# Repacking the small products ahead of a recurrence: strips on TensorE, projections by mixed blocks, another order of banks

## The reference, cut to what matters

```python
# block 1: cross-attention over 375 context rows, 16 heads of 32, and an MLP of 2048
hidden = softmax(q @ k.T * scale) @ v @ cproj_w + cproj_b + x
x = hidden + gelu(layer_norm(hidden) @ fc_w + fc_b) @ proj_w + proj_b
# block 2
xa = _ln(x, ln1_w, ln1_b)
sx = previous row of xa - xa
xxx = tanh((xa + sx * maa_x) @ maa_w1).reshape(b, l, 5, 32)
xxx = einsum('blfd,fde->blfe', xxx, maa_w2)
xm = xa + sx * (maa_stack + xxx)
xk, xw, xv, xr, xg = the five of xm
w = exp(-exp(time_decay + tanh(xw @ td_w1) @ td_w2))      # td_w1: 512 x 64
r, k, v = xr @ Wr.T, xk @ Wk.T, xv @ Wv.T
g = silu(xg @ Wg.T)
# 32 heads of 16: out_t = r_t (u k_t v_t + s), s = k_t v_t + w_t s
x1 = x + group_norm(out) * g @ Wo.T
rr = sigmoid(xr2 @ Wfr.T); kk = square(relu(xk2 @ Wfk.T))  # xk2, xr2: mixes of ln(x1)
return x1 + rr * (kk @ Wfv.T)
```

## Time and profile before

| | |
|---|---|
| median of 3 runs | 1780.87 us |
| the profiled execution | 1791.03 us, span 1789.2 us |
| mean granted TensorE clock | 0.969 |
| TensorE busy | 1697.5 us (95%) |
| VectorE busy | 1167.6 us (65%) |
| ScalarE (ACT) busy | 657.2 us (37%) |
| GpSimd (POOL) busy | 281.2 us (16%) |

### The profile page before, as it was taken

One profiled execution on the slowest core, in us unless ns is written; L12 is line 12 of the kernel. 1 busy time (PEld: TensorE's weight loads), 2 busy tenths in 40 slices (PEclk: granted clock), 3 DMA queues, 4 the chain that ended last, 5 costly groups with the idle time before them and its releaser, 6 DMA issues.

```text
span 1789.2 us, 18450 instructions
## 1 busy us (share of the span) xinstructions
PE 1697.5 (95%) x6792; PEld 860.0 (48%) x6792; DVE 1167.6 (65%) x1620; ACT 657.2 (37%) x1507; POOL 281.2 (16%) x377
## 2 busy tenths in 40 slices
PE   6999999899999999999999999999989999999968
PEld 3555544345555444445555444455544445444423
DVE  1233200336999895548997965389989767999841
ACT  2466420124666222236663213256532135313111
POOL 1100000122121001121220002211200023136020
PEclk9999999889999999989999999999999999999989
DMA  7001012124111123351120232520022415232131
GB/s 254 12 29 52 1 52 90 50 83 141 37 45 54 41 93 127 97 159 37 37 62 22 88 114 89 157 78 9 16 76 78 135 52 159 85 118 74 56 101 44
DMA packets 75143, 138.82 MB, mean 78 GB/s; under 512 B 16624, under 2 KB 26736, under 8 KB 75056
## 3 DMA queue, kind: packets, MB, share of 16 engines
q1 hardware_dynamic: 60064, 102.36, 17.8%
q0 software_dynamic: 11776, 31.70, 6.0%
q10 hardware_dynamic: 3216, 3.60, 0.7%
HBM read 113.78 MB, written 23.86 MB: 77 GB/s over the span
## 4 chain that ended last, share of the span: by engine, by line
PE 82%; DVE 11%; issue 3%; ACT 3%; ACTq 1%; POOL 0%; DVEq 0%; POOLq 0%
PE bank L324 55%; PE bank L511 12%; PE bank L366 4%; PE bank L358 3%; PE bank L596 3%; DVE C L1315 2%; PE bank L378 2%; DVE sm L1252 1%; PE bank L631 1%; PE bank L346 1%; DVE C L1323 1%; DVE YB L1332 1%; PE bank L610 1%; DVE C L1307 1%; ACT XA L988 1%
## 5 line engine op out<-in xcount | busy, mean ns | idle before, releaser
L1315 DVE TENSOR_TENSOR_SCAN C<-XA,C 128x896 f32<-128x896 f32 x112 | 228.8, 2043 | 3.2
L511 PE MATMUL bank<-ring,HT 128*112 128x512 f32 x512 | 222.3, 592 | 0.0
L1252 DVE CUSTOM_DVE_ANT_0 sm<-bank,maskb 112x375 f32<-112x375 f32 x256 | 124.4, 542 | 139.0 <-PE bank L358 138.5
L324 PE MATMUL bank<-ctx_t,Wk 128*128 128x375 f32 x512 | 200.1, 517 | 14.3 <-DMA Wk<-in_wk 11.3
L324 PE MATMUL bank<-C,ring 128*128 128x448 f32 x512 | 209.2, 565 | 1.4 <-ACT Wk L988 1.4
L324 PE MATMUL bank<-SX,ring 128*128 128x448 f32 (+2 forms) x544 | 195.9, 519 | 4.1 <-issue 4.1
L324 PE MATMUL bank<-Wv,ctx_t 128*125 128x512 f32 x384 | 180.9, 596 | 0.4 <-ACT C L988 0.4
L366 PEld LDWEIGHTS bank<-ident,sm 112*125 112x125 f32 x768 | 124.8, 191 | 106.5 <-ACT sm L1003 44.1
L1009 ACT ACTIVATE probT<-bank 125x336 f32<-125x336 f32 x256 | 114.1, 446 | 164.3 <-PE bank L366 162.7
L1003 ACT ACTIVATE sm<-sm,nm 112x375 f32<-112x375 f32 x256 | 153.4, 599 | 3.3 <-DVE nm L1252 3.1
L511 PEld LDWEIGHTS bank<-ring,HT 128*112 128x112 f32 x512 | 90.6, 177 | 127.2 <-issue 127.2
(11 more groups left out here) (166 smaller groups left out, 2156.3 us busy)
## 6 DMA issues: line engine op xcount, KB each, us to landing
ring<-in_stream SPq DMA_DIRECT2D x64, 1024.0 KB, 5.2
ctx_t<-in_ctxT SPq DMA_DIRECT2D x16, 750.0 KB, 4.7
rkw_scratch<-HT POOLq DMA_DIRECT2D x48, 224.0 KB, 3.1
rkw<-rkw_scratch POOLq DMA_DIRECT2D x24, 224.0 KB, 3.2
HT<-in_x SPq DMA_DIRECT2D x16, 224.0 KB, 5.5
X<-in_x SPq DMA_DIRECT2D x16, 224.0 KB, 5.1
v_scratch<-HT POOLq DMA_DIRECT2D x16, 224.0 KB, 2.7
VB<-v_scratch SPq DMA_DIRECT2D x4, 896.0 KB, 4.5
```

Of the source, the lines that this page charges most:

```text
L324: last_ = nc.tensor.matmul(out_ap, pairs[k][0], pairs[k][1], start=(k == 0), stop=(k == len(pairs) - 1))
L511: last_ = nc.tensor.matmul(bank[SC[b]][0:LQ, :], HT[:, c, b * LQ:(b + 1) * LQ], w[:, c, :], start=(m == 0 and c == 0), stop=(m == 3 and c ...
L1252: nc.vector.tensor_tensor_reduce(out=sm[0:LQ, slot, :], in0=tile(name)[0:LQ, 0:LK], in1=maskb[:, n % 2, :], scale=-SCALE, scalar=3.0e38, o ...
L1315: own.step(nc.vector.tensor_tensor_scan(out=part, data0=wrep[:, i % 2, :], data1=part, initial=0.0, op0=ALU.mult, op1=ALU.add))
```

## The change

- W1 is cut into 80 products of 32 output rows by 112 columns: for each of the five factors j the four sequences go to four column strips of the array and lie under one another in one bank. The tanh is five instructions of 128 x 112 into TA.
- `low_rank(j)` is 16 products (4 sequences in 4 row strips, 4 blocks of channels), of 112 columns, with one bank for each sequence. `maa_w2` is repeated four times down the partitions; three of its five factors are loaded for each group by SP into memory lent by `sm` or `qT`.
- TD and DC go in two strips of 64, each with 224 columns.
- VectorE scales in 16 pieces of 112 columns for a mix. Mixes 0, 2 and 3 (k, v, r) are finished block by block, each with a signal of its own. The mixes lie in C[0], GT, C[1], GT, C[0].
- P1, P2 and P3 (`by_blocks`) run over the blocks of channels outside and the four results inside, in four banks at once, with LR1, LR2, the decay's products, LR3 and LR4 between the blocks. The order of banks is set anew at the start of each stage, and `skip` jumps over four.
- The decays are staged in EW, the memory of YB, and have a semaphore of their own, `w_out`; k is stored before them.
- The zeroing of YB is gone, and the first step's product goes there directly.
- In group 3, `last_norm(0)` and `last_cols(0)` come after P3's copies, those of part 1 after P4, and VectorE does `last_mixes(0)` after all five mixes and `last_mixes(1)` at i == 2 of the scan. GpSimd's `last_std(0)` comes before the first loads of the scan and `last_std(1)` behind them.

```diff
-ORDER = [1, 0, 2, 3, 4]
+ORDER = [0, 1, 2, 3, 4]
+BY_BLOCKS = [True, False, True, True, False]
+MIX0, MIXED, MIXES = 1, [5, 9, 10, 14, 18], 18
...
-        TD = GT[0:DD, 0, :]
-        TA = sm[:, :, :].rearrange("p s t -> p (s t)")[:, 0:T]
-        TB = sm[0:DM, :, :].rearrange("p s t -> p (s t)")[:, T:2 * T]
+        TA = sm[:, :, :].rearrange("p s t -> p (s t)")[:, 0:5 * LQ]
+        lent = [sm[:, :, :].rearrange("p s t -> p (s t)")[:, 5 * LQ:]] * (NG - 1) + [
+            qT[:, :, :].rearrange("p e t -> p (e t)")]
+        mw2c = [r[:, 0:3 * D].rearrange("p (j n) -> p j n", j=3) for r in lent]
+        TD = [r[:, 3 * D:3 * D + T // 2] for r in lent]
+        mixed = [C[0], GT, C[1], GT, C[0]]
+        EW = YB[:, :, :].rearrange("p j t -> p (j t)").rearrange("p (e t) -> p e t", e=E)
...
+            def any_first():
+                first = turn_of["wide"] + 1
+                any_order[:] = [*SC, *(WIDE[(first + k) % 4] for k in range(4))]
+                turn_of["any"] = -1
...
             def pre(g):
-                k = any_bank()
+                any_first()
+                k1 = [any_bank() for j in range(5)]
                 for c in range(E):
-                    pe.wait_ge(mix_ready, g * 9 + c + 1)
-                    last_ = product(bank[k][:, 0:T], [(mw1[:, c_, 0:P], C[1][:, c_, :]) for c_ in range(E)], c, c + 1)
+                    pe.wait_ge(mix_ready, g * MIXES + MIX0 + c)
+                    for j in range(5):
+                        q = ORDER[j]
+                        for b in range(GB):
+                            last_ = nc.tensor.matmul(bank[k1[j]][DM * b:DM * (b + 1), 0:LQ],
+                                                     mw1[:, c, DM * q:DM * (q + 1)], C[1][:, c, b * LQ:(b + 1) * LQ],
+                                                     start=(c == 0), stop=(c == E - 1))
...
                 def low_rank(j):
+                    evacuated(pe, ("W1", g, j))
+                    k = [any_bank() for b in range(GB)]
                     for e in range(E):
+                        for b in range(GB):
+                            rows = slice(DM * b, DM * (b + 1))
+                            last_ = nc.tensor.matmul(bank[k[b]][:, e * LQ:(e + 1) * LQ], w[rows, e * P:(e + 1) * P],
+                                                     TA[rows, j * LQ:(j + 1) * LQ], start=True, stop=True)
+                            if e == E - 1:
+                                closed(last_, ("LR", g, j, b), k[b])
...
+                def by_blocks(j, between):
+                    at = (0, 2, 3)[j - 1]
+                    w, k = weights(g, PRE_P[j - 1]), [any_bank() for e in range(E)]
+                    for c in range(E):
+                        pe.wait_ge(mix_ready, g * MIXES + MIXED[at] + c)
+                        for e in range(E):
+                            last_ = nc.tensor.matmul(bank[k[e]][:, 0:T], w[:, c, e * P:(e + 1) * P],
+                                                     mixed[at][:, c, :], start=(c == 0), stop=(c == E - 1))
+                            if c == E - 1:
+                                closed(last_, ("P", g, j, e), k[e])
+                        if c in between:
+                            between[c]()
+                    piece_done(g, PRE_P[j - 1])
...
                 low_rank(0)
+                by_blocks(1, {0: lambda: low_rank(1), 2: lambda: skip(4, lambda: low_rank(2))})
+                decay_hidden()
+                by_blocks(2, {0: decay, 2: lambda: skip(4, lambda: low_rank(3))})
+                by_blocks(3, {0: lambda: low_rank(4)})
+                if g == NG - 1:
+                    last_cols(0)
+                if g != NG - 2:
+                    w, late = weights(g, PRE_P[3]), g < NG - 1
+                    pe.wait_ge(mix_ready, g * MIXES + MIXED[4])
+                    channels_out([("P", g, 4, e) for e in range(E)], w, mixed[4], any_bank, hi=E - late)
+                if g == NG - 1:
+                    last_cols(1)
...
+                if g < NG:
+                    ready(sp, ("T", g * GB + GB - 1, E - 1, HQ - 1))
+                    sp.dma_start(mw2c[g], maa_w2[2:5, :, :].rearrange("j p n -> p j n")).then_inc(mw_in, 16)
...
                 for e in range(E):
                     evacuated(pool, ("P", g, 2, e))
                     store(g, 3, e)
+                if g == NG - 1:
+                    last_std(0)
+                pool.wait_ge(w_out, 64 * (g + 1))
                 for e in range(E):
-                    pool.wait_ge(e_out[e], 64 * g + 32)
+                    pool.wait_ge(e_out[e], 48 * g + 16)
                 load_first(g, 1, rkw_in)
                 load_first(g, 2, rkw_in)
+                if g == NG - 1:
+                    last_std(1)
...
-                    prod = nc.vector.tensor_tensor(S[:, :, :], S[:, :, :], r.unsqueeze(1).to_broadcast([P, RS, LQ]),
-                                                   ALU.mult)
-                    if last:
+                    prod = nc.vector.tensor_tensor((S if last or i > 0 else YB)[:, :, :], S[:, :, :],
+                                                   r.unsqueeze(1).to_broadcast([P, RS, LQ]), ALU.mult)
+                    if last or i == 0:
...
+                def scaled(j, e):
+                    for b in range(GB):
+                        name = ("LR", g, j, b)
+                        ready(dve, name)
+                        last_ = nc.vector.scalar_tensor_tensor(
+                            out=mixed[j][:, e, b * LQ:(b + 1) * LQ], in0=tile(name)[:, e * LQ:(e + 1) * LQ],
+                            scalar=col(f"maa_{ORDER[j]}", e), in1=SX[:, GB * e + b, :], op0=ALU.add, op1=ALU.mult)
...
                     for e in range(E):
+                        scaled(j, e)
+                        if BY_BLOCKS[j]:
+                            added(j, e).then_inc(mix_ready, 1)
...
-                    elif g == NG - 1 and j > 2:
-                        last_mixes(j - 3)
-                if g < NG - 1:
-                    own.step(nc.vector.memset(YB[:, :, :], 0.0))
-                    for unit in range(in_mixes(g)):
-                        scan_unit(g, unit)
+                if g == NG - 1:
+                    last_mixes(0)
+                for unit in range(in_mixes(g)):
+                    scan_unit(g, unit)
...
-                        if i in (7, 8):
+                        if i == 2:
+                            last_mixes(1)
+                        elif i in (7, 8):
```

More of the change, by code:

```diff
@@ L601, in pre @@
-                low_rank(0)
-                low_rank(1)
-                low_rank(2)
-                pe.wait_ge(mix_ready, g * 9 + 5)
-                k = any_bank()
-                closed(product(bank[k][0:DD, 0:T], [(tw1[:, c, :], C[0][:, c, :]) for c in range(E)]), ("TD", g), k)
-                evacuated(pe, ("TD", g))
-                for e in range(E):
-                    k = any_bank()
-                    closed(nc.tensor.matmul(bank[k][:, 0:T], tw2[:, e * P:(e + 1) * P], TD, start=True, stop=True),
-                           ("DC", g, e), k)
@@ L612, in pre @@
-                for j in range(1, 4 if g == NG - 2 else 5):
-                    if 2 < j + 1 < 5:
-                        low_rank(j + 1)
-                    if g == NG - 1 and j in (2, 3):
-                        last_cols(j - 2)
-                    w = weights(g, PRE_P[j - 1])
-                    pe.wait_ge(mix_ready, g * 9 + j + 5)
-                    late = j == 4 and g < NG - 1
-                    channels_out([("P", g, j, e) for e in range(E)], w, C[j % 2], any_bank, hi=E - late)
+                    pe.wait_ge(mix_ready, g * MIXES + MIX0 + c)
@@ new lines, in decay_hidden @@
+                def decay_hidden():
+                    pe.wait_ge(mix_ready, g * MIXES + MIXED[1])
+                    k = any_bank()
+                    for c in range(E):
+                        for h in range(2):
+                            last_ = nc.tensor.matmul(bank[k][DD * h:DD * (h + 1), 0:T // 2], tw1[:, c, :],
+                                                     mixed[1][:, c, h * (T // 2):(h + 1) * (T // 2)],
+                                                     start=(c == 0), stop=(c == E - 1))
+                    closed(last_, ("TD", g), k)
@@ new lines, in decay @@
+                def decay():
+                    evacuated(pe, ("TD", g))
+                    k = [any_bank() for e in range(E)]
+                    for e in range(E):
+                        for h in range(2):
+                            rows, to = slice(DD * h, DD * (h + 1)), k[2 * (e // 2) + h]
+                            last_ = nc.tensor.matmul(bank[to][:, (e % 2) * (T // 2):(e % 2 + 1) * (T // 2)],
+                                                     tw2[rows, e * P:(e + 1) * P], TD[g][rows, :],
+                                                     start=True, stop=True)
+                            if e % 2:
+                                closed(last_, ("DC", g, e // 2, h), to)
@@ L1139, in pre @@
             def pre(g):
```

(32 more changed lines are left out.)

131 lines of the change are left out of this document (64 added, 67 removed).

## The result

The changed kernel takes 1759.97 us, the median of four runs (1756.24 to 1763.45), beside 1780.66 for the kernel before on the same chip (1778.77 to 1786.08): a ratio of 0.9873, with a 95% interval of 0.9843 to 0.9902. The forecast, 1759 us, is within a microsecond of it.

What follows compares the result with a forecast made beforehand. It took TensorE's order of work as the bound, and VectorE's scan in the last group. Gains of 16.0 + 12.2 + 13.0 less 12.2 make 29 us; less 6.8 for low clock, 22 off the median 1780.87: 1759, range 1744 to 1775.

Steps and rivals of the forecast that it cites:

- The price of a packed product: On TensorE: a packed low-rank product of 32 passes takes 1.1 us, where it took 3.0 before.
- The stage: Group 1, W1's start to the next attention's first score: 65.6 us instead of 77.8, gain 12.2.
- the last 40 passes take 1.0: 3.9 us from W1's start: W1 on TensorE: last mix block there after about 2.8 us, W1 done at 3.9; with W1B 7.7 before.
- the charge of 1.7 us of low clock a stage: All four stages: one stretch at the 1.2 GHz level each, costing 1.7 us, 6.8 together.
- Group 0: Group 0's stage: 67.9 us instead of 83.9, gain 16.0, with W1 taking 6.9 at low clock.
- The queues: Loads and stores: SP's new 768 KB load and the decays' staging cost nothing; without cover about 5 us a group.
- The last group: Group 3: scan starts 5.0 us later and last_mixes(1) adds 7.2 inside it, loss 12.2.
- Outside the stages: Attention and MLP between the stages: a gain of 0.
- (c): Packed products: strips load one after another, a low-rank product takes 3.5 us, not 1.1; total 1807; chance 0.06.
- (a): Stages: clock stays at 1.2 GHz through P1, two more stretches a stage, 14 us, total 1772; chance 0.14.
- (b): Last group: late rkw load or VectorE stretched by GpSimd, another 12 to 17 us, 1771 to 1776; chance 0.08.
- (d): Stages: no low stretch, inserts changing over at half price, scaling 0.2 apart; about 12 us better, 1747; chance 0.12.

Runs made afterwards that it cites:

- late_v: Changed kernel with the 1 MB ring load of P2's weights held until LR0 is done: 1750.81 us, ratio 0.9802 to the kernel before.
- best: Changed kernel with the edits of late_v and early_cols together: 1742.23 us, ratio 0.9759 to the kernel before.
- one_strip: Changed kernel with all four sequences' low-rank products in the first strip of 32 rows: 1839.17 us, ratio 1.0295 to the kernel before.
- no_between: Changed kernel with the low-rank and decay products moved from between the blocks to behind each projection: 1849.97 us, ratio 1.0356 to the kernel before.
- lr_twice: Changed kernel with every packed low-rank product issued twice: 1773.01 us, ratio 0.9929 to the kernel before.
- filler: Changed kernel with four thrown-away full-width products between LR0 and P1: 1757.20 us, ratio 0.9835 to the kernel before.
- early_cols: Changed kernel with the last group's statistics, normalisation, columns and transposes for part 0 taken earlier: 1751.49 us, ratio 0.9807 to the kernel before.
- mixes_first: Changed kernel with last_mixes(1) moved out of the last group's scan to before it: 1770.69 us, ratio 0.9915 to the kernel before.
- best_fill: best plus thrown-away products in group 0's waits at the border and before W1: 1738.97 us, ratio 0.9738 to the kernel before.

## Why the prediction was right

*The bound and the chain.* Right. TensorE's order held what I took from it, and in the last group the scan's start and VectorE's gapless scan held the rest.

*The price of a packed product*, 1.1 us: 1.09, and 0.9 of it passes. W1 at 0.96 us a block: 160 passes in 4.29 us, 27 ns each, and 4.23 from W1's start to LR0 where nothing holds it up (`late_v`), for 3.9. The Trainium skill, TensorE: Matmul & The Clock Gate, "Wait — 56ns, not 53.3ns?", gives about 62 ns for each matmul with hardware decode off, by which W1 would take an estimated 9.9 us; the runs don't show it.

*The stage.* Counted from LR0, group 1: P1 at 3.1 us (forecast 3.1), LR1 at 7.9 (7.6), LR2 at 15.2 (15.0), P2 at 22.0 (22.0), P3 at 38.3 (38.35), P4 at 51.7 (51.9), the first score at 60.8 (61.65). The mixes of VectorE are the reason why so much agrees: 1.06 for four pieces and 0.62 to add is 1.63 a block, for the 1.65 taken.

*Two terms were wrong and cancelled, by luck.* W1 takes 6.4, 5.9 and 5.9 us in groups 1 to 3, not 3.9: the step "the last 40 passes take 1.0: 3.9 us from W1's start" looked at VectorE and at the passes alone, and the instructions' own fetch beside a ring load cost another 1.3 to 1.9 us. Against it stands the charge of 1.7 us of low clock a stage. The stretch came, at P1's first block, but it cost 0.6: the block ended 4.8 instead of 3.1 us after its start, and LR1 behind it had 1.4 us to wait in any case (1.0 in `late_v`, none here). In group 1 the two leave 67.1 us against 65.6 + 1.7 = 67.3.

*Group 0* gained 4 us more than the sum with its clock: 1.4 as W1 took 5.5 us from its start, not 6.9 (the clock rose at 344.4 and not at 349), 1.7 as no stretch of low clock lay in the stage behind W1, and 1.0 from there to the first score. That W1 met the full clock early is luck too: it took 5.9 us in the second trace of the changed kernel and 6.7 in `best`.

*The queues.* Right that SP's new load would cost nothing: LR2, the first to need it, starts without a wait (718.46). The staging of the decays in the sum buffer was priced at nothing and wasn't tried by itself; nor were the strips of W1 and of the decay's products, or the dropped zeroing. In group 3 the repeat of the decays waited 0.28 us for its rkw load, where I had put the load ahead by 0.5. But I had followed SP's loads by when their data are wanted, and never by what else they hold up while they run; that is how the hole in W1 stayed out of the sum.

*The last group.* Scan 5.0 us later by the sum, 6.2 measured (W1 is 2.0 over its forecast, 1.5 of that its hole); the mixes 7.2 in the scan, which is 7.3 longer.

*Outside the stages.* I gave nothing to attention and MLP, and 6.1 us came from there: 1.7, 1.65 and 2.8. The first two are one stretch of low clock less where attention begins: none behind group 0 for 3.4 us at 430.8 before, and 3.4 us at 767.7 for 6.8 at 799.5. The forecast held all the same, since it took 22 us off the median and the medians are 21 apart. Between the traces it was 35, of which 28 in the stages and the scan, where the sum had 22. So the sum is right to 6 us, and that 1759 came within one is luck; the executions of the kernel before on this chip lie between 1778.8 and 1791.0 us, and the profiled one is the slowest of them, which makes the traces' difference the larger one.

*The rivals.* (c) is excluded: 1.09 us against 3.75 in one strip. (a) did not come: groups 0 to 2 have one stretch behind W1 at most, and group 3, besides P1's, one of 6.8 us at 1453.8, over transposes and P4, where the scan didn't wait for TensorE. Its sign, low clock over P1, came in part, over one block of four in groups 1 to 3; `one_strip` and `no_between` show that it was a real danger (183 and 190 us of low clock). (b) did not come in its size. (d) needed the low stretch gone: `late_v` is that case, with a ratio of 0.9802, 1745 us on the first chip.

## What to carry to other kernels

Products of 32 rows belong four to a round, each in its own strip, but count their instructions too: a run of some 290 short ones (143 passes and their weight loads) in 4 us outran the instruction fetch when a large load ran beside it, and here the load could be issued 7 us later at no cost. Between dependent blocks, put independent products where the wait is and work out what each wait becomes if the insert is gone; the added waits of `no_between` cost their 17 us a stage and then 9 more in clock. When a change makes one engine's work shorter, look in the last stage for the chain that nobody hid, and move its first step, not its last.

## What the runs showed of the hardware

- A load of 1 MB over all DMA engines (85% busy) kept a 16 KB fetch of TensorE's instructions back by 2 us: 3.3 us into W1 instead of 1.2. TensorE went on 1.2 to 1.4 us after the fetch had landed.
- The clock follows small changes: eight kernels that differ by a few us of TensorE's work or waits (the changed one, `lr_twice`, `late_v`, `filler`, `early_cols`, `mixes_first`, `best`, `best_fill`) had between 61 and 108 us at the 1.2 GHz level, and the changed one 91 and 101 in its two traces. An edit that shortens one wait can change the clock in a stage far from it, so gains under 5 us could be read only stage by stage.
- In four column strips 160 passes of 112 columns took 4.29 us, 27 ns each, and in four row strips 32 took 1.16; I had priced both near that from attention's rows. In a single strip of 32 rows the same 32 passes cost 3.4 times as much.
